# A transformer stage woven in a new order: attention output on its own counter, two tiles' ranks in another bank

## The reference

```
x = x + _L0_ffn_ref(_layernorm(x), ...)       # ternary product          stage_c
x = x + _L1_xattn_ref(_layernorm(x), ctx, ...)  # 16 heads of 16          keys_values, scores, softmax, mix
x = x + _L1_attn_ref(_layernorm(x), ...)      # relu(q k)^2 v, gated      stage_e
x = x + _L1_ffn_ref(_layernorm(x), ...)       # top 8 of 160, experts     stage_f, then experts()
```

## Time and profile before

| | |
|---|---|
| median of 3 runs (range) | 1385.31 us (1382.23 to 1386.63) |
| the profiled execution: time, span | 1384.27 us, 1381.1 us |
| first part, second part, third part | up to 476, to 1005.3, to 1381.1 us |
| busy in the span | PE 1244.3, DVE 946.3, ACT 605.4, POOL 548.0 us |
| granted TensorE clock, mean | 0.954 |

### The profile page before, as it was taken

One profiled execution on the slowest core, in us unless ns is written; L12 is line 12 of the kernel. 1 busy time (PEld: TensorE's weight loads), 2 busy tenths in 40 slices (PEclk: granted clock), 3 DMA queues, 4 the chain that ended last, 5 costly groups with the idle time before them and its releaser, 6 DMA issues.

```text
span 1381.1 us, 34814 instructions
## 1 busy us (share of the span) xinstructions
PE 1244.3 (90%) x11693; PEld 897.9 (65%) x11693; DVE 946.3 (69%) x2728; ACT 605.4 (44%) x1761; POOL 548.0 (40%) x717
## 2 busy tenths in 40 slices
PE   5999999999998689999999999997848999999946
PEld 3667667767766356767776767775636776667725
DVE  2477666666666436787778887777637777777737
ACT  2445555455454156667667677665301111111140
POOL 1011110101100101556666666656616776667730
PEclk8999999999999779999999999999979999999969
DMA  9322323233323000111122111113298899898659
GB/s 308 99 98 90 133 91 138 93 133 108 133 80 106 32 16 16 37 65 53 57 64 73 57 65 54 64 38 103 91 263 254 257 267 279 262 265 253 207 211 368
DMA packets 124879, 185.73 MB, mean 134 GB/s; under 512 B 23285, under 2 KB 90516, under 8 KB 122784
## 3 DMA queue, kind: packets, MB, share of 16 engines
q10 hardware_dynamic: 57376, 77.19, 17.6%
q1 hardware_dynamic: 51200, 71.66, 16.9%
q0 software_dynamic: 16128, 34.67, 7.1%
HBM read 190.88 MB, written 78.25 MB: 195 GB/s over the span
## 4 chain that ended last, share of the span: by engine, by line
PE 43%; ACT 5%; ACTq 5%; DMA 4%; DVE 4%; issue 4%; POOL 1%; SPq 0%; DVEq 0%; POOLq 0%
PE bank L1038 5%; PE bank L1063 5%; PE bank L485 4%; ACT ex L472 3%; PE bank L1023 3%; PE bank L457 3%; ACTq L951 2%; PE bank L663 2%; PE bank L525 2%; PE bank L592 2%; PE bank L614 2%; PE bank L240 2%; PE bank L256 2%; PE bank L1050 1%; PE bank L433 1%
## 5 line engine op out<-in xcount | busy, mean ns | idle before, releaser
L1073 POOL DMA_INDIRECT y_d<-y,xg x208 | 204.0, 981 | 121.1 <-DVE y L1069 85.2
L1043 ACT ACTIVATE ex<-bank 128x256 f32<-128x256 f32 x104 | 40.0, 384 | 278.6 <-PE bank L1038 118.3
L773 POOL DMA_INDIRECT xs_d<-xw,slot_id x128 | 134.3, 1049 | 30.2 <-issue 29.3
L472 ACT ACTIVATE ex<-bank,nmC 128x256 f32<-128x256 f32 x256 | 119.2, 483 | 14.2 <-DVE nmC L466 13.8
L1069 DVE COPY y<-bank 128x512 f32<-128x512 f32 x104 | 71.9, 691 | 70.5 <-PE bank L1063 63.4
L485 PE MATMUL bank<-ident,ex 128*128 128x128 f32 x512 | 79.2, 284 | 20.0 <-ACT ex L472 16.6
L485 PEld LDWEIGHTS bank<-ident,ex 128*128 128x128 f32 x512 | 61.8, 145 | 54.3 <-ACT ex L472 21.1
L1023 PE MATMUL bank<-ident,xg 128*128 128x128 f32 x416 | 70.0, 292 | 19.4 <-DMA xg<-xs_d 19.4
L466 DVE TENSOR_REDUCE nmC<-bank 128x2 f32<-128x512 f32 x128 | 82.8, 680 | 5.7 <-PE bank L457 4.8
L1337 POOL TENSOR_TENSOR stB<-stB,small 128x1 f32<-128x1 f32 x32 | 20.3, 634 | 165.3 <-DVE stB L1334 165.3
L1027 DVE COPY ex<-bank 128x512 f32<-128x512 f32 x104 | 71.5, 687 | 21.0 <-PE bank L1023 16.3
(11 more groups left out here) (393 smaller groups left out, 3314.1 us busy)
## 6 DMA issues: line engine op xcount, KB each, us to landing
xs_d<-zeros ACTq DMA_DIRECT2D x16, 1768.0 KB, 7.4
pTC<-in_wexp ACTq DMA_DIRECT2D x104, 256.0 KB
xg<-xs_d SPq DMA_DIRECT2D x310, 68.0 KB
cT<-in_ctx SPq DMA_DIRECT2D x32, 512.0 KB, 4.0
wh<-in_wexp ACTq DMA_DIRECT2D x52, 256.0 KB
cT<-in_wexp ACTq DMA_DIRECT2D x52, 256.0 KB
kTC<-in_wexp ACTq DMA_DIRECT2D x52, 256.0 KB
vvC<-in_wexp ACTq DMA_DIRECT2D x52, 256.0 KB
```

The costliest lines, as they stand in the source:

```text
L472: last = act.activation(ex[:, u, 256 * b:256 * b + 256], bank[hp][:, 256 * b:256 * b + 256], ACT.Exp, bias=nm[:, u, b:b + 1], accum_out=su ...
L773: pool.indirect_dma_start(out=xs_d, out_offset=bass.IndirectOffsetOnAxis(ap=slot_id[z][:, k:k + 1], axis=0), in_=xw[z][:, k, :], in_offset ...
L1073: pool.indirect_dma_start(out=y_d, out_offset=bass.IndirectOffsetOnAxis(ap=who, axis=0), in_=y[:, n, g, :], in_offset=None, bounds_check=l ...
```

## The change

Three edits. `ORDER2` has new numbers for all steps. The events of `mix` count on a new letter M and no more on D, on which scores and softmax stay, so that scores of tile i+1 may stand ahead of the product of tile i. And the ranks of the last two tiles go into bank 3, which the scores have left by then, so that `qk` of tile 15 waits for `lge` of tile 14 and not for its `spot`; for that the shared expert's `common_up` has one bank instead of two, and each round waits for the activation of the round before.

```diff
-    "scores0": (171.27,),
+    "scores0": (-9.08073,),
-    "mix": (212.81, 213.57, 216.24, 219.28, 221.57, 223.09, 224.24, 226.52, 229.19),
+    "mix": (33.44092, 13.86743, 31.61789, 33.92874, 54.05327, 35.28207, 41.82809, 55.17324, 60.14257,),
...
-        C, D, E, F, R, G, H = turns
+        C, D, E, F, R, G, H, M = turns
         V, W, Y = (Count(nc, sem, n) for n in ("common_turn", "common_up", "common_down"))
+
+        LAST = range(TILES - 2, TILES)
...
             C.wait(pe, "qx", i - 1)
-            D.wait(pe, "norm", i - 2)
+            M.wait(pe, "norm", i - 2)
...
-            D.done(i, "pe", last, "pv")
-            yield
-            D.wait(act, "recT", i)
-            D.wait(act, "norm", i - 1)
-            D.done(i, "act", act.copy(recT[:, :], bank[5][:, :]), "recTe")
+            M.done(i, "pe", last, "pv")
+            yield
+            M.wait(act, "recT", i)
+            M.wait(act, "norm", i - 1)
+            M.done(i, "act", act.copy(recT[:, :], bank[5][:, :]), "recTe")
...
             E.wait(pe, "xT", j)
-            R.wait(pe, "spot", j - 1)
+            if j - 1 in LAST:
+                F.wait(pe, "lge", j - 1)
+            else:
+                R.wait(pe, "spot", j - 1)
...
-            rank, after = bank[7][:, 0:EXPERTS], bank[7][:, 256:256 + EXPERTS]
+            if j in LAST:
+                rank, after = bank[3][:, 0:EXPERTS], bank[3][:, 256:256 + EXPERTS]
+                D.wait(pe, "e7", TILES - 1)
+                R.wait(pe, "spot", j - 1)
+            else:
+                rank, after = bank[7][:, 0:EXPERTS], bank[7][:, 256:256 + EXPERTS]
...
                 V.wait(pe, "act", n)
-                W.wait(pe, "act", n - 2)
+                W.wait(pe, "act", n - 1)
                 for c in range(2):
-                    last = pe.matmul(bank[2 + n % 2][:, 0:DIM], wgs[:, c, :], ex[:, n % 2, c * DIM:(c + 1) * DIM], start=(c == 0), stop=(c == 1))
+                    last = pe.matmul(bank[2][:, 0:DIM], wgs[:, c, :], ex[:, n % 2, c * DIM:(c + 1) * DIM], start=(c == 0), stop=(c == 1))
```

More of the change, by code:

```diff
@@ L75 @@
[L75 to L81, removed]
@@ L469, in softmax @@
             D.wait(act, f"pT{u}", i - 1)
-            D.wait(act, f"rec{m}", i - 1)
+            M.wait(act, f"rec{m}", i - 1)
             for b in range(2):
@@ L479, in softmax @@
             elif u == 0:
-                D.wait(pe, "norm", i - 1)
+                M.wait(pe, "norm", i - 1)
                 C.wait(pe, "qx", min(i + 1, TILES - 1))
@@ L489, in softmax @@
             D.wait(eng, f"pT{u}", i)
-            D.wait(eng, "pv", i - 1)
+            M.wait(eng, "pv", i - 1)
             D.done(i, en, copy(pT[:, u, :], bk[:, :]), f"pT{u}e")
@@ L497, in mix @@
                 D.wait(dve, [f"e{4 * m + u}" for u in range(4)], i)
-                D.wait(dve, f"recx{m}", i - 1)
-                D.done(i, "dve", dve.reciprocal(rec[:, 4 * m:4 * m + 4, :], sums[:, 4 * m:4 * m + 4, :]), f"rec{m}")
+                M.wait(dve, f"recx{m}", i - 1)
+                M.done(i, "dve", dve.reciprocal(rec[:, 4 * m:4 * m + 4, :], sums[:, 4 * m:4 * m + 4, :]), f"rec{m}")
                 yield
-                D.wait(pool, f"rec{m}", i)
-                D.wait(pool, "recT", i - 1)
+                M.wait(pool, f"rec{m}", i)
+                M.wait(pool, "recT", i - 1)
                 for b in range(2):
@@ L506, in mix @@
                                               bc(half[:, :].rearrange("p (o n) -> p o n", o=1), 1, 4), ALU.mult)
-                D.done(i, "pool", last, f"recx{m}")
+                M.done(i, "pool", last, f"recx{m}")
             yield
-            D.wait(pe, ("recx0", "recx1"), i)
+            M.wait(pe, ("recx0", "recx1"), i)
             D.wait(pe, "pT7e", i)
@@ L513, in mix @@
                     last = pe.transpose(bank[5][:, (2 * m + b) * P:(2 * m + b + 1) * P], recx[:, m, b, :], ident[:, :])
-            D.done(i, "pe", last, "recT")
+            M.done(i, "pe", last, "recT")
             yield
@@ L551, in stage_e @@
             yield
-            D.wait(dve, "yp", j)
+            M.wait(dve, "yp", j)
             C.wait(dve, "xb", j)
@@ L874, in common_up @@
                 Y.wait(act, "pe", n - 2)
-                W.done("act", act.activation(ex[:, 4, n % 2 * DIM:n % 2 * DIM + DIM], bank[2 + n % 2][:, 0:DIM], ACT.Silu))
+                W.done("act", act.activation(ex[:, 4, n % 2 * DIM:n % 2 * DIM + DIM], bank[2][:, 0:DIM], ACT.Silu))
         def common_down():
@@ L880, in common_down @@
                 if n == 0:
-                    D.wait(pe, "norm", TILES - 1)
+                    M.wait(pe, "norm", TILES - 1)
                     H.wait(pe, "x4", TILES - 1)
```

63 lines of the change are left out of this document (35 added, 28 removed).

## The result

The changed kernel takes 1401.59 us (median of 4 runs, 1400.82 to 1402.36), the kernel before beside it 1385.97. The ratio is 1.011, with a 95% interval of 1.0081 to 1.0138. The forecast was 1376.0, faster: wrong in sign, and 10.6 us outside the range. The profiled execution took 1402.35 with a span of 1400.6.

A forecast was written before the change was run, and what follows sets the result against it. PE bounds the kernel before; after the change a closed ring through POOL's DMAs was to decide. 1384.27 us with -13.8 - 11.2 + 4.8 + 7.3 + 4.6 = -8.3 gave 1376.0, range 1361 to 1391.

The forecast's parts named there:

- Start: Tiles 0 to 2 and the start of s0 of tile 0: 76.0 us against 87.24, so -11.2.
- About 5 us of it is no gain: Of the gain in tiles 0 to 2, about 5 us is only s0 moved ahead, paid back at the end.
- Middle: The twelve tiles from s0 of tile 3 to s0 of tile 15: 340.8 us against 354.64, so -13.8.
- The ring: Closed chain through POOL's eight DMAs, powers, DVE's norms and spot chain; summed to 28.45, taken as 28.4 us a tile.
- the low clock: Lower granted clock cost PE 5.8 us over the twelve tiles; forecast to cost nothing more than the rounding.
- s0 to pv of tile 15: Last tile, from its scores to its attention product: 25.4 us against 20.57, so +4.8.
- pv to yo of tile 15: Last tile, from attention product to yo, behind tile 14's leftover work: 33.3 us against 26.0, so +7.3.
- yo of tile 15 to the table: From yo of the last tile to the page table, before 27.95 us: logits and ranks later, together +4.6.
- The two gains set against these: After yo of tile 15: last DVE steps in one piece (-1.3), page keys not held up on PE (-1.1).
- Rival 3: DMA issue in one piece slowed by DVE: eight take 12.7 us instead of 10.2, total 1405 us; chance 0.15.
- Rival 1: PE remains the bound in the middle at 27.5 us a tile, total 1365 us; chance 0.17.
- Rival 2: DMAs 1.4 us apart and slower POOL give 29.1 us a tile, other terms 0: 1384 us, no change; chance 0.20.

The follow-up runs named there:

- b4: Changed kernel with each tile's eight scatter DMAs spread four, two, two instead of in one piece: 1395.84 us beside 1385.20, ratio 1.007.
- b2: Changed kernel with only the bank edit undone (ranks in bank 7, ups in two banks): 1393.67 us beside 1385.20, ratio 1.005.
- b3: Changed kernel with the shared expert's rounds 4 to 7 moved behind the ranks of tile 15: 1398.89 us beside 1385.20, ratio 1.0092.
- a1: Kernel before with only the separate attention counter added, order and banks unchanged: 1499.73 us beside 1500.62, ratio 0.9998.
- f1: Changed kernel with bank edit undone, shared expert's rounds off the path of logits and ranks, scatters spread: 1377.91 us beside 1386.16, ratio 0.9947.

## Why the prediction was wrong

By its own steps, forecast against measured. The table was to end 8.3 us earlier and ended 16.4 later; of these 24.7 us the largest parts are the middle (9.7) and the stretch from yo of tile 15 to the table (10.2).

- **Start, -11.2.** By its own cut it was right (-11.6, and s0 of tile 0 1.3 earlier). The step that failed is the sentence behind it: "About 5 us of it is no gain". It was 11 us, as the slot numbers of tile 3 show (1.8 ahead). I measured the gain at the first step of a tile and left the payment to the terms of the end, where it was sized too small.
- **Middle, -13.8.** Measured -4.1. The ring closes where the forecast put it: PE waits 1.38 before xnT, DVE's xn waits 0.79 for the power, and s0 no longer waits. But the term has two parts. The ring at 28.4 against 29.07 a tile was to give 8.0 us; it runs at 29.14 and gives nothing (+1.7 over the twelve tiles). Most of the 0.7 a tile is in the links from xn to XN. The other 5.8 us were the low clock ("I let it cost nothing more than the rounding"): that came true, with 1.00 in all twelve tiles. So the step that failed is the ring's sum, and the 4.1 us gained are not what the new order was meant to give.
- **s0 to pv of tile 15, +4.8.** Measured +9.8, at a granted clock of 0.77; h alone took 3.62 us in it. The count had no term for the clock. b4 has the same order on PE here and a clock of 0.94, h takes 1.88, and the stretch 27.4 us instead of 30.3: 2.9 of the 5.0 us missed go with the clock.
- **pv to yo of tile 15, +7.3.** Measured +9.0. The second up waits 2.5 us for the activation of the first, a table load in it, where the whole pair was put at 1.6; the ranks of tile 14 then wait 3.45 for sel.
- **yo of tile 15 to the table, +4.6.** Measured +14.8, the largest miss. "xfT and lg stand behind more rounds of up and down (+0.7)" was 7.5: two ups in one bank, at the lower clock, and the wait for an activation with a table load ahead of it. b2 shows 6.3 of it to come with the bank edit, the clock's part included. For ez and the ranks behind round 4 the forecast was 3 + 3.3 = 6.3 and the rows give 6.0; b3 took back 4.9. The two gains set against these (-1.3 and -1.1) did not come: from the ranks to the table's end it took 20.1 us, 18.9 before, where 16.5 was counted.
- **Rival 3**, the only slower one, had the sign and not the mechanism. It wanted DMAs 1.62 us apart; they are 1.29 apart. The Trainium skill (SBUF — State Buffer, "SBUF: two separate sides") has GpSimd and VectorE exclude each other on a shared port pair; no row here shows the DMAs lengthened by it: their median was 972 ns, 1000 before. **Rival 1** (PE bound, 27.5) fell with the 29.14, and b4 shows that 27.5 was out of reach even without the ring (28.65). **Rival 2** had the ring's length (29.1) but not its reason (DMAs 1.4 apart), and put the other terms at 0 in sum, where they came to +20.6.
- **The table loads** were priced right: 1.28 us each. The Trainium skill (ScalarE activation tables: per-element evaluation and per-set limits, "What a function is on this engine") gives 1283 ns between two functions of different sets; the traces agree. That the new places make five of three was in the forecast too; what was missed is how long PE stands queued behind them.

What is shown: the counter does nothing in the old order (a1, beside 1500); the bank edit costs 7.9 us in this order (b2); the piece of eight scatters holds the middle by 0.5 us a tile (b4); bank and places together cost 17.9 (b4 against f1, taken beside different kernels before, 1385.20 and 1386.16, which makes it 18.9). What is only argued: how the 10 us of the places divide among queueing, table loads and the lower clock in which the end runs.

## What to carry to other kernels

Measure a reordering of a pipelined loop at a late step of the iteration as well as an early one: a lead at the first step that is missing at the last is depth, and the drain pays for it. When a mean over many iterations changes, split it by the granted clock first: here twelve tiles got 4.1 us shorter and a tile at full clock did not. In the drain, the last tiles with nothing behind them, check for each filler on an in-order engine what it waits for; an up product that needs an activation is no filler in front of the last logits. A buffer edit that removes a covered wait can cost more through the buffer that it takes.
